# Attention part of a recurrence-plus-experts kernel: row roots one tile sooner, result additions in two pairs

## The chip, the cores and the metric

One core of a Trainium2 chip runs the whole program. Its engines are TensorE (PE in the profile, its weight loads PEld), VectorE (DVE), ScalarE (ACT), GpSimd (POOL) and SyncE (SP), each with its own queue of instructions. They meet at semaphores. PSUM holds what TensorE writes, SBUF the rest. The metric is the device time of one execution in microseconds (us).

## The reference, cut to what matters

The input x is 2 sequences of 1024 rows of 256 values, fp32. A row normalisation gives xn, and the result adds two functions of it to x:

```python
xn = _layernorm(x)
x = x + _L0_attn_ref(xn, ...) + _L0_ffn_ref(xn, ...)

def _L0_attn_ref(hidden_states, ...):
    ...                                   # a gated recurrence over time, in logarithms -> log_h
    log_h = (log_h - log_h.mean()) / jnp.std(log_h, ddof=1)
    h = jnp.exp(log_h)[:, 1:, :]
    x = h + hidden_states
    mu = x.mean(axis=-1, keepdims=True)
    var = x.var(axis=-1, keepdims=True)
    return (x - mu) * jax.lax.rsqrt(var + LN_EPS) * ln_w + ln_b

def _L0_ffn_ref(hidden_states, ...):
    ...                                   # softmax over 8 experts, each row keeps 2 of them
    for e in range(NUM_EXPERTS):
        h = jax.nn.silu(x @ w1[e].T) * (x @ w3[e].T)
        out = out + h @ w2[e].T * expert_weight
```

The last three lines of the attention part, the normalisation of the rows of h + xn, are what this change is about.

## The kernel before

**Tiles.** Each row goes to two experts. The (row, expert) pairs are sorted by expert into tiles of 128 rows, numbered from 0; between 33 and 39 tiles can be needed, 36 are here (0 to 35). Every engine walks the same tiles in a loop written out by hand for j = 1 to 32, with the attention work hung into given tiles, and then a nest of conditions (`tail`) for tiles 33 and up. The weights of an expert are split into a high and a low part. They come in four pieces: SyncE loads a piece, ScalarE rounds it to the high part (line 604), POOL subtracts to get the low part (line 424). Up to two pieces fall to a tile, by a plan computed at the start.

**One tile j on each engine.** TensorE: up products (`up`, line 1296), transposes of the next tile's rows (line 1265), in tiles 20 to 27 also transposes of a part of h (`h_back`, line 1354), down products of tile j - 1 (line 1314), transposes of the gated values (`h_tile`, line 1326, after the gate). ScalarE: silu (line 595), high part of the next rows (line 572), scaling copy of the down products of tile j - 1 out of PSUM (`y_copy`, line 621), high part of the gated values (`h_hi`, line 590), then the pieces. VectorE: `gate` (line 961, two products), low part of the next rows (line 952, the up products of tile j + 1 wait for it), `slot_weight` (line 1067), the hook `between(j)`, `h_lo` (line 956, the second half of the down products waits for it), the hook `after(j)`. `h_lo(j)` runs when the up products of tile j + 1 have already begun.

**The attention rows.** In tiles 20 to 27 VectorE adds h to xn, two groups of 128 rows to a step, and takes their mean and variance (`row_stats`). ScalarE takes square roots for four steps at a time (`row_deviations`, wrapped in two loads of an activation table, lines 696 and 704), in the second half of tiles 24 and 28. VectorE takes reciprocals (`row_scales`) in tiles 25 and 29 and runs `last_norm(m)`, m = 0 to 7, in `after` of tiles 25 to 32: four products of 128x256, two on line 1054 and two on line 1059, all operands in SBUF. They raise the semaphore s_p2 by 2.

**Adding into the result.** The result buffer starts as a copy of x. POOL adds to it: for every tile a `scatter` (line 406) of the 128 scaled rows, after `y_copy`, and four times `add_attention` (line 413), a plain transfer of 512 normalised rows that adds. Scatters and additions can touch the same rows, so each waits for all before it: `rows_added` waits for the scatters (s_st) and for the additions so far (s_ab). A tile on POOL is: the gather of the rows of tile j + 4 (line 390), the scatter of tile j - 1, then the pieces of tile j. The additions stand ahead of POOL's tiles 27, 29 and 31 and behind tile 32. The last tile's scatter is at line 467, after its own copy (line 725).

**End of TensorE's work.** Ahead of the last down products stand twelve products of constants (`warm(LAST_FILL)`, line 1176), whose result nobody reads.

Of the kernel before, what the change touches and what calls it, by code (L numbers as in the profile page):

```python
# [14 lines left out]
P = 128  # L15
# [11 lines left out]
SURE = 2 * NTOK // P + 1  # L27
# [18 lines left out]
SPLIT = 512  # L46
WARM = 96
FILL = 8
LAST_FILL = 12
BIG = 3.0e38  # L50


def build_program(nc, x, small, w_main, w_tail, out, xn_dram):
# [5 lines left out]
    with ctx:  # L59
# [285 lines left out]
        def _(pool):  # L345
# [47 lines left out]
            def rows_added(j, parts):  # L393

                if j:
                    pool.wait_ge(s_st, 16 * j)
                if j == 0:
                    pool.wait_ge(s_fill, 16)
                if parts:
                    pool.wait_ge(s_ab, 16 * parts)  # L400
# [5 lines left out]
                pool.indirect_dma_start(out, bass.IndirectOffsetOnAxis(sidx[:, j:j + 1], 0),  # L406
                                        ysb[:, j % DEEP, :], None, compute_op=ALU.add).then_inc(s_st, 16)

            def add_attention(j, m):

                pool.wait_ge(s_p2, 4 * m + 4)
                rows_added(j, m)
                pool.dma_start(out[4 * m * P:4 * (m + 1) * P, :].rearrange("(t p) d -> p t d", p=P),
                               xn[:, 4 * m:4 * m + 4, :], accum_op=ALU.add).then_inc(s_ab, 16)

            def split_due(before, j):

# [26 lines left out]
            for i in range(8):  # L444
                done = pool.value_load(plan[0:1, ds(LOOP * i + 1, 1)], min_val=0, max_val=PIECES * (E - 1))
                for u in range(LOOP):
                    j = LOOP * i + 1 + u
                    if j in (27, 29, 31):
                        add_attention(j - 1, added)
                        added += 1  # L450
                    done = tile(i, u, done, added)
            add_attention(SURE - 1, added)

            def drain(j):
                if j + DEEP < NTILES:
# [18 lines left out]
        def _(act):  # L474
# [171 lines left out]
            def row_deviations(h):  # L646
                act.wait_ge(s_p1, 3 * (4 * h + 4))
                act.activation(std[:, 8 * h:8 * h + 8], mv[:, 8 * h:8 * h + 8, 1], ACT.Sqrt,
                               bias=eps[:, :]).then_inc(s_std3, 1)
# [33 lines left out]
            def roots(j):  # L683
                if j == 18:
                    deviation()
                else:
                    row_deviations((j - 24) // 4)

            def tile(i, u, done=None, table=None, first=None, second=None):

# [18 lines left out]
            for i in range(8):  # L709
                done = act.value_load(plan[0:1, ds(LOOP * i + 1, 1)], min_val=0, max_val=PIECES * (E - 1))  # L710
                for u in range(LOOP):
                    j = LOOP * i + 1 + u
                    if j in (3, 4, 5, 6, 7, 10, 11, 12, 13, 19, 20):
                        done = tile(i, u, done, "natural_log_exp_and_others", exp_log_first, exp_log_second)
                    elif j in (18, 24, 28):
                        done = tile(i, u, done, "sqrt_and_others", None, roots)
                    else:
                        done = tile(i, u, done)
# [11 lines left out]
        def _(dve):  # L730
# [303 lines left out]
            def row_stats(m):  # L1034
                rows = xn[:, 2 * m:2 * m + 2, :]
                dve.wait_ge(s_htr, m + 1)
                dve.tensor_tensor(rows, tr_ps.rearrange("p (t d) -> p t d", t=2), rows, ALU.add).then_inc(s_p1, 1)
                dve.wait_ge(s_p1, 3 * m + 1)
                for t in range(2):
                    ins = dve.bn_stats(st3[:, t, :], xn[:, 2 * m + t, :])  # L1040
                ins.then_inc(s_p1, 1)
                dve.wait_ge(s_p1, 3 * m + 2)
                for t in range(2):
                    ins = dve.bn_aggr(mv[:, 2 * m + t, :], st3[:, t, :])
                ins.then_inc(s_p1, 1)

            def row_scales(h):
                dve.wait_ge(s_std3, h + 1)
                dve.reciprocal(rstd[:, 8 * h:8 * h + 8], std[:, 8 * h:8 * h + 8]).then_inc(s_rs3, 1)
                dve.wait_ge(s_rs3, h + 1)  # L1050

            def last_norm(m):
                for t in range(2 * m, 2 * m + 2):
                    ins = dve.scalar_tensor_tensor(xn[:, t, :], xn[:, t, :], mv[:, t, 0:1], lnwb[:, 0, :],  # L1054
                                                   ALU.subtract, ALU.mult)
                ins.then_inc(s_p2, 1)
                dve.wait_ge(s_p2, 2 * m + 1)
                for t in range(2 * m, 2 * m + 2):
                    ins = dve.scalar_tensor_tensor(xn[:, t, :], xn[:, t, :], rstd[:, t:t + 1], lnwb[:, 1, :],  # L1059
                                                   ALU.mult, ALU.add)  # L1060
                ins.then_inc(s_p2, 1)
# [31 lines left out]
            def between(j):  # L1093
                if j == 1:
                    less_n(0)
                if j == 2:
                    less_n(2)
                if j in (4, 5, 6, 7):
                    add_half(j // 2, 1 - j % 2)
                if j == 3:  # L1100
                    run_max(0)
                if j in (8, 9):
                    run_max(j - 6)
                if j in (10, 12):
                    run_scan(j - 10)
                if 13 <= j <= 16:
                    plus_max(j - 13)
                if 20 <= j <= 27:
                    row_stats(j - 20)

            def after(j):
                if j == 1:
                    add_l3(1)
                    less_n(1)
                if j == 2:
                    less_n(3)
                if j == 3:
                    max_steps(0)
                    less_max(0)
                if j == 4:  # L1120
                    run_max(1)
                if j == 5:
                    max_steps(1)
                    less_max(1)
                if j == 6:
                    add_l3(2)
                    add_l3(3)
                if j == 7:
                    less_l2(2)
                    less_l2(3)  # L1130
                if j in (8, 9):
                    max_steps(j - 6)
                    less_max(j - 6)
                if j in (11, 12):
                    run_scan(1 if j == 11 else 3)
                if 13 <= j <= 16:
                    logh(j - 13)
                    if j < 16:
                        log_stats(j - 13)
                    else:  # L1140
                        sums()
                if j == 17:
                    squares()
                if j == 18:
                    normaliser()
                if j in (25, 29):
                    row_scales((j - 25) // 4)
                if 25 <= j <= 32:
                    last_norm(j - 25)

            def tile(i, u, hooks=False):

# [18 lines left out]
        def _(pe):  # L1171
# [215 lines left out]
                    tile(i, u, True)  # L1387

            def last_down(used):
                warm(LAST_FILL)  # L1390
                down(used - 1, pe.snap(r_before, min_val=0, max_val=E - 1))
            tail(pe, tile, last_down)

# [37 lines left out]
```

## Time and profile before

| | us |
|---|---|
| median of 3 runs | 357.22 (357.09 to 359.14) |
| profiled execution | 357.79 |
| its span (first to last event in the profile) | 356.1 |
| TensorE busy | 325.8 (91%) |
| VectorE busy | 260.8 (73%) |
| ScalarE busy | 219.9 (62%) |
| POOL busy | 206.4 (58%) |
| mean granted clock of TensorE | 0.969 |

The page shares the span out over the chain of work that ended last: 54% of it is TensorE, 23% VectorE, 8% ScalarE, 2% transfers. In 40 slices of the span TensorE is busy 70% or more in the first 38, some 30% in the next and not at all in the last. The kernel moves 37.00 MB, 11.97 of them through POOL's queue.

### The profile page before, as it was taken

How to read it: one execution, taken by the hardware profiler on the slowest of the kernel's cores; microseconds unless marked ns; L12 is line 12 of the kernel's file. 1: busy time of each engine (PE TensorE's matmuls, PEld its weight loads, DVE VectorE, ACT ScalarE, POOL GpSimd, SP SyncE). 2: the span in 40 equal slices, each digit the busy share in tenths (PEclk: the TensorE clock that was granted, in tenths of full speed). 3: DMA queues.
4: the chain of work that ended last, by engine and by line, in shares of the span. 5: the costliest groups of instructions: out<-in, count | busy, mean ns of one | idle time of the engine just before them, and what ended most of it. 6: DMA issues, size and time to landing. Idle time of an engine off the chain costs nothing.

```text
span 356.1 us, 6682 instructions
## 1 busy us (share of the span) xinstructions
PE 325.8 (91%) x1964; PEld 273.9 (77%) x1964; DVE 260.8 (73%) x466; ACT 219.9 (62%) x328; POOL 206.4 (58%) x137
## 2 busy tenths in 40 slices
PE   8998999799999999999898999999999999979830
PEld 8883464588878898997787899889898988969730
DVE  5488787989996899889899842584589668763300
ACT  2547997455879974999854269934853485323400
POOL 4500023159968674989899728563885475945331
PEclk9999969989999999999999999999999999999985
DMA  7924912005444542354354434542463534354621
GB/s 263 426 120 137 293 52 59 15 11 150 122 82 115 142 101 32 80 129 129 44 144 109 102 38 115 142 101 33 84 181 89 75 45 76 47 76 49 98 38 15
DMA packets 19086, 37.00 MB, mean 104 GB/s; under 512 B 2272, under 2 KB 13536, under 8 KB 19008
## 3 DMA queue, kind: packets, MB, share of 16 engines
q0 software_dynamic: 9168, 11.97, 21.5%
q1 hardware_dynamic: 8496, 22.56, 20.4%
q10 hardware_dynamic: 1376, 1.85, 1.4%
q8 instruction: 29, 0.48, 0.6%
q14 instruction: 17, 0.14, 0.1%
HBM read 27.45 MB, written 11.03 MB: 108 GB/s over the span
## 4 chain that ended last, share of the span: by engine, by line
PE 54%; DVE 23%; ACT 8%; issue 8%; DMA 2%; ACTq 1%; POOL 1%; POOLq 0%; DVEq 0%
PE PS L1296 23%; PE PS L1314 11%; PE PS L1190 6%; PE PS L1326 5%; DVE wrow L1067 3%; DVE tmp L961 3%; PE PS L1176 2%; DMA out<-work,sidx 2%; DVE hT L956 2%; DVE U L985 2%; DVE A L998 1%; PE PS L1220 1%; DVE xrow L1054 1%; DVE xrow L1059 1%; PE PS L1265 1%
## 5 line engine op out<-in xcount | busy, mean ns | idle before, releaser
L1296 PE MATMUL PS<-wbuf,xT 128*128 128x512 f32 (+1 forms) x648 | 149.6, 384 | 4.9 <-issue 3.7
L1296 PEld LDWEIGHTS PS<-wbuf,xT 128*128 128x128 f32 x648 | 118.3, 190 | 29.4 <-issue 9.3
L424 POOL TENSOR_TENSOR wbuf<-raw,wbuf x28 | 81.4, 2924 | 23.1 <-ACT wbuf L604 21.4
L406 POOL DMA_INDIRECT out<-work,sidx x35 | 62.7, 1792 | 53.2 <-ACT work L621 20.1
L1314 PE MATMUL PS<-wbuf,hT 128*128 128x256 f32 x648 | 86.8, 288 | 0.0
L1314 PEld LDWEIGHTS PS<-wbuf,hT 128*128 128x128 f32 x648 | 79.3, 189 | 1.9 <-issue 1.9
L390 POOL DMA_INDIRECT work<-xn_dram,gidx x39 | 50.4, 1292 | 51.8 <-DVE gidx L892 36.1
L595 ACT ACTIVATE tmp<-PS 128x512 f32<-128x512 f32 x72 | 32.0, 460 | 41.6 <-PE PS L1296 41.3
L961 DVE TENSOR_TENSOR tmp<-tmp,PS 128x512 f32<-128x512 f32 x72 | 35.0, 516 | 29.4 <-ACT tmp L595 28.6
L956 DVE TENSOR_TENSOR hT<-PS,hT 128x768 fp32r<-128x768 f32 x36 | 34.2, 949 | 29.3 <-ACT hT L590 24.2
L621 ACT ACTIVATE work<-PS,wrow 128x256 f32<-128x256 f32 x35 | 16.4, 470 | 38.0 <-PE PS L1314 38.0
L1067 DVE SCALAR_TENSOR_TENSOR wrow<-work,first_pick 128x1 f32<-128x1 f32 x37 | 37.1, 1003 | 0.0
L1326 PE MATMUL PS<-ident,tmp 128*128 128x128 f32 x216 | 30.1, 275 | 5.7 <-DVE tmp L961 5.6
L590 ACT ACTIVATE hT<-PS 128x768 fp32r<-128x768 f32 x35 | 28.4, 810 | 10.4 <-PE PS L1326 10.4
L1190 PE MATMUL PS<-xnT_M,small_sb 128*128 128x512 f32 x64 | 32.3, 646 | 1.0 <-ACT tmp L525 1.0
L604 ACT ACTIVATE wbuf<-raw x28 | 30.4, 1110 | 4.0 <-issue 3.9
L1326 PEld LDWEIGHTS PS<-ident,tmp 128*128 128x128 f32 x216 | 24.0, 141 | 7.9 <-DVE tmp L961 6.9
L1190 PEld LDWEIGHTS PS<-xnT_M,small_sb 128*128 128x128 f32 x64 | 12.6, 208 | 14.1 <-issue 12.9
L704 ACT ACT_TABLE_LOAD x14 | 18.0, 1283 | 0.3
L696 ACT ACT_TABLE_LOAD x14 | 18.0, 1283 | 0.3
L952 DVE TENSOR_TENSOR xT<-PS,xT 128x256 fp32r<-128x256 f32 x37 | 15.5, 419 | 0.1
L572 ACT ACTIVATE xT<-PS 128x256 fp32r<-128x256 f32 x37 | 14.0, 381 | 1.7 <-PE PS L1265 1.7
(185 smaller groups left out, 350.7 us busy)
## 6 DMA issues: line engine op xcount, KB each, us to landing
raw<-w_main SPq DMA_DIRECT2D x24, 544.0 KB
raw<-w_main SPq DMA_DIRECT2D x8, 416.0 KB
xn_dram<-xrow SPq DMA_DIRECT2D x4, 516.0 KB, 7.2
out<-xrow POOLq DMA_DIRECT2D x4, 512.0 KB, 6.1
xrow<-x SPq DMA_DIRECT2D x4, 256.0 KB, 4.8
xrow<-x ACTq DMA_DIRECT2D x4, 256.0 KB, 5.4
small_sb<-small ACTq DMA_DIRECT2D x1, 768.0 KB, 7.9
work<-xn_dram,gidx POOLq DMA_INDIRECT x39
```

The costliest lines, as they stand in the source:

```text
L390: pool.indirect_dma_start(xg[:, k, :], None, xn_dram, bass.IndirectOffsetOnAxis(gidx[:, j:j + 1], 0)).then_inc(s_gt[k], 16)
L406: pool.indirect_dma_start(out, bass.IndirectOffsetOnAxis(sidx[:, j:j + 1], 0), ysb[:, j % DEEP, :], None, compute_op=ALU.add).then_inc(s_s ...
L424: pool.tensor_tensor(lo, raw[:, ds(part, WP)], hi.bitcast(fp32), ALU.subtract).then_inc(s_w, 1)
L595: act.activation(sls[n], w1_ps[n], ACT.Silu).then_inc(s_silu, 1)
L604: act.activation(wslot(p // PIECES + 1, 0, part), raw[:, ds(part, WP)], ACT.Copy).then_inc(s_hi, 1)
L956: dve.tensor_tensor(hT[:, 1, :], hT_ps, hT[:, 0, :].bitcast(fp32), ALU.subtract).then_inc(s_hlo, 1)
L961: dve.tensor_tensor(g_hs[n], sls[n], w3_ps[n], ALU.mult).then_inc(s_g, 1)
L1067: dve.scalar_tensor_tensor(wrow[:, j:j + 1], xg[:, k, D:D + 1], first_pick[:, j:j + 1], xg[:, k, D + 1:D + 2], ALU.mult, ALU.max).then_inc ...
L1190: ins = pe.matmul(PS[:, base + qo * CH:base + (qo + 1) * CH], wzh_sb[:, q, mat, qo * P:(qo + 1) * P], xnT[:, q, c * CH:(c + 1) * CH], star ...
L1296: ins = pe.matmul(PS[:, at:at + cols], xT[:, slot, xpart, q * P:(q + 1) * P], wbuf[:, w, wpart, q * 2 * F + at:q * 2 * F + at + cols], sta ...
L1314: ins = pe.matmul(y_ps, hT[:, hpart, c * P:(c + 1) * P], wbuf[:, w, wpart, W13 + c * D:W13 + (c + 1) * D], start=(c == 0 and hpart == 0 an ...
L1326: ins = pe.transpose(hT_ps[:, c * P:(c + 1) * P], g_h[:, a:a + P], ident[:, :])
```

## The change

The roots, reciprocals and `last_norm` steps 0 to 5 move one tile forward. Step 6 goes into `between(30)`, ahead of `h_lo(30)`, and step 7 into `after(30)`. Tiles 31 and 32 carry no step any more. POOL issues the additions in two pairs, ahead of its tiles 28 (steps 0 to 3) and 31 (steps 4 to 7), each pair with one wait in front and none between; the addition behind tile 32 goes. The twelve constant products go.

```diff
-LAST_FILL = 12
...
-            def add_attention(j, m):
-
-                pool.wait_ge(s_p2, 4 * m + 4)
-                rows_added(j, m)
-                pool.dma_start(out[4 * m * P:4 * (m + 1) * P, :].rearrange("(t p) d -> p t d", p=P),
-                               xn[:, 4 * m:4 * m + 4, :], accum_op=ALU.add).then_inc(s_ab, 16)
+            def add_attention(j, first):
+
+                pool.wait_ge(s_p2, 4 * first + 8)
+                rows_added(j, first)
+                for m in (first, first + 1):
+                    pool.dma_start(out[4 * m * P:4 * (m + 1) * P, :].rearrange("(t p) d -> p t d", p=P),
+                                   xn[:, 4 * m:4 * m + 4, :], accum_op=ALU.add).then_inc(s_ab, 16)
...
-                    if j in (27, 29, 31):
+                    if j in (28, 31):
                         add_attention(j - 1, added)
-                        added += 1
+                        added += 2
                     done = tile(i, u, done, added)
-            add_attention(SURE - 1, added)
...
-                    row_deviations((j - 24) // 4)
+                    row_deviations((j - 23) // 4)
...
-                    elif j in (18, 24, 28):
+                    elif j in (18, 23, 27):
                         done = tile(i, u, done, "sqrt_and_others", None, roots)
...
                 if 20 <= j <= 27:
                     row_stats(j - 20)
+                if j == 30:
+                    last_norm(6)
...
-                if j in (25, 29):
-                    row_scales((j - 25) // 4)
-                if 25 <= j <= 32:
-                    last_norm(j - 25)
+                if j in (24, 28):
+                    row_scales((j - 24) // 4)
+                if 24 <= j <= 29:
+                    last_norm(j - 24)
+                if j == 30:
+                    last_norm(7)
...
             def last_down(used):
-                warm(LAST_FILL)
                 down(used - 1, pe.snap(r_before, min_val=0, max_val=E - 1))
```

## Rows read from the trace of the kernel before

**Rows 1.** Timeline, last 35 us: start, length, engine, line, operation, [idle before <-releaser].

```profile
322.67 1.58 POOL L406 DMA_INDIRECT out<-work,sidx  x1 [1.26 <-DMA out<-work,sidx]
...
327.09 1.38 POOL L413 DMA_DIRECT2D out<-xrow  x1 [2.84 <-DMA out<-work,sidx]
...
333.73 1.64 POOL L406 DMA_INDIRECT out<-work,sidx  x1 [3.88 <-issue]
...
338.99 0.84 PE L1176 MATMUL PS<-ones_b 128*128 128x128 bf16 x12 [2.32 <-issue]
...
342.11 0.47 ACT L725 ACTIVATE hst<-PS,wrow 128x256 f32<-128x256 f32 x1 [3.61 <-PE PS L1314]
343.00 1.56 POOL L406 DMA_INDIRECT out<-work,sidx  x1 [2.44 <-DMA out<-work,sidx]
...
347.79 1.57 POOL L467 DMA_INDIRECT out<-hst,scol  x1 [2.67 <-DMA out<-work,sidx]
```

**Rows 2.** Timeline: POOL's weight pieces (L424) and VectorE's products beside them.

```profile
265.97 3.23 DVE L1059 SCALAR_TENSOR_TENSOR xrow<-xrow,rstd,small_sb 128x256 f32<-128x256 f32 x2
265.99 2.53 POOL L424 TENSOR_TENSOR wbuf<-raw,wbuf  x1 [0.57 <-issue]
...
289.39 5.24 POOL L424 TENSOR_TENSOR wbuf<-raw,wbuf  x2
...
308.10 3.12 POOL L424 TENSOR_TENSOR wbuf<-raw,wbuf  x1
308.15 3.75 DVE L1054 SCALAR_TENSOR_TENSOR xrow<-xrow,mv,small_sb 128x256 f32<-128x256 f32 x2
```

**Rows 3.** Timeline: up products (L1296) of tiles 26, 27, 30, 32, 33; gate; normalisation.

```profile
262.77 4.10 PE L1296 MATMUL PS<-wbuf,xT 128*128 128x512 f32 x18
...
269.12 0.94 DVE L961 TENSOR_TENSOR tmp<-tmp,PS 128x512 f32<-128x512 f32 x2
...
270.86 4.11 PE L1296 MATMUL PS<-wbuf,xT 128*128 128x512 f32 x18
...
280.16 0.87 DVE L1054 SCALAR_TENSOR_TENSOR xrow<-xrow,mv,small_sb 128x256 f32<-128x256 f32 x2
...
292.13 4.12 PE L1296 MATMUL PS<-wbuf,xT 128*128 128x512 f32 x18
...
306.15 4.11 PE L1296 MATMUL PS<-wbuf,xT 128*128 128x512 f32 x18
...
315.85 4.10 PE L1296 MATMUL PS<-wbuf,xT 128*128 128x512 f32 x18 [1.50 <-issue]
```

**Rows 4.** Timeline: copies (ACT L621), scatters (L406) and gathers (L390) of tiles 22 to 34.

```profile
247.81 0.47 ACT L621 ACTIVATE work<-PS,wrow 128x256 f32<-128x256 f32 x1 [2.17 <-PE PS L1314]
...
249.09 1.58 POOL L406 DMA_INDIRECT out<-work,sidx  x1 [4.41 <-ACT work L621]
...
277.79 0.47 ACT L621 ACTIVATE work<-PS,wrow 128x256 f32<-128x256 f32 x1 [2.17 <-PE PS L1314]
...
288.02 1.57 POOL L406 DMA_INDIRECT out<-work,sidx  x1 [2.55 <-DMA out<-work,sidx]
...
305.74 1.01 POOL L390 DMA_INDIRECT work<-xn_dram,gidx  x1 [0.17 <-DVE wrow L1067]
...
307.05 1.58 POOL L406 DMA_INDIRECT out<-work,sidx  x1 [0.30 <-issue]
```

**Rows 5.** Windows: length, busy by engine (x instructions), granted clock, DMA share, GB/s.

```profile
70.00:71.00 1.00, 0.45 (x2) 0.41 (x3) 0.97 (x2) 0.00 (x0) 0.00 (x0) 1.00 0.00 0
...
70.55:76.21 5.66, 5.66 (x18) 4.38 (x18) 0.70 0.01 3
278.16:282.25 4.09, 4.09 (x18) 3.23 (x18) 1.00 0.84 144
```

In the first of these the engines are PE, PEld, DVE, ACT and POOL; the other two count the up products (L1296) of tiles 1 and 28 alone, on PE and PEld.

**Rows 6.** Window while one addition (L413, issued at 327.09) moves.

```profile
331.00:331.50 0.50, 0.50 (x3) 0.39 (x3) 0.50 (x1) 0.00 (x0) 0.00 (x0) 1.00 1.22 197
```

**Rows 7.** Page, groups by line: h_lo, count, busy us and mean ns.

```profile
L956 DVE TENSOR_TENSOR hT<-PS,hT 128x768 fp32r<-128x768 f32 x36 | 34.2, 949 | 29.3 <-ACT hT L590 24.2
```

## The prediction

> **What bounds the kernel now.** I read the chain of waits first, then the timeline of the last 110 us engine by engine, then parts of that stretch in windows. From tile 20 on the kernel is a chain of tiles of about 7 us on TensorE: the up products of tile 28 begin at 278.16 [rows 5] and those of tile 30 at 292.13 [rows 3], two tiles in 13.97. In the last 14 us it is another chain. POOL adds rows to the result one transfer at a time, each waiting for the one before. The last partial attention transfer goes out at 327.09, the next scatter only at 333.73, and from there scatter follows scatter until the last one at 347.79 [rows 1]. Tile 35, the last, was copied out of PSUM by 342.11 + 0.47 = 342.58 [rows 1], so its rows lie 5.2 us waiting for their turn. That gap is what the change can win.
>
> The second thing to see is how VectorE and POOL block each other. POOL's subtraction for a weight piece (line 424) ran from 265.99, and beside it two products of the last normalisation (line 1059) took 3.23, where two of the same size (line 1054 at 280.16 [rows 3]) took 0.87. At 308.10 and 308.15 the same: line 1054 stood until the piece was done, 3.75 for its two products [rows 2]. Both kinds of instruction read two SBUF operands; VectorE products with one operand in PSUM ran through such a piece undisturbed. So every step of the normalisation that falls on a piece costs up to 3.1 us of VectorE time. The gate (line 961) of the next tile is queued behind it, the transposes wait for the gate, and TensorE for both: U(j), the start of the up products of tile j, came 270.86 - 269.12 = 1.74 after that gate began [rows 3]. Before, this cost about 8.09 - 7.30 = 0.8 in tile 26 (262.77 to 270.86, where the next tile took 7.30 [rows 3, 5]), and in tile 32 (306.15 to 315.85, 9.70, of which 1.50 is another wait [rows 3]) 9.70 - 6.98 - 1.50 = 1.2.
>
> **The change part by part.** *Roots one tile sooner.* ScalarE's two table loads and the root move from tiles 24 and 28 to 23 and 27. Nothing is added. In tile 23 they stand in front of two weight pieces, as they do in tile 28 now, and there the up products of tile 30 show no wait [rows 3]. I cost this at 0; what covers it is the transposes of h that TensorE does in tile 24. If that cover failed, the gate of tile 24 would be late, and I bound it by what a late gate cost in tile 26, 0.8.
>
> *Normalisation one step sooner.* Step 0 moves from tile 25 to 24, where no piece is running. Step 1 then stands where step 0 stood, against the piece at 265.99. I carry the 0.8 of tile 26 over: 0 change, bounds -0.8 (it misses) and +1.0 (three of its four products remain, not two).
>
> *Two pieces at a time, ahead of tile 28.* On POOL the wait moves from tiles 27 and 29 to tile 28. Behind it in POOL's queue stand the gather of tile 32, the scatter of tile 27 and, behind these, the two weight pieces of tile 28, which before ran at 289.39 [rows 2]. Their new time:
> - The copy of tile 26 ends at 277.79 + 0.47 = 278.26, and a scatter follows its copy by 249.09 - 248.28 = 0.81 [rows 4]: 279.07.
> - An add follows the scatter it waits for by 327.09 - 322.67 = 4.42 [rows 1]: 283.49. Step 3 of the normalisation, which it waits for too, is done by 282.
> - The next scatter follows one add by 333.73 - 327.09 = 6.64 [rows 1]. No row shows two adds. Below, the second hides altogether (6.64 in all); above, both stand in line (13.3). While one add moves, the windows show 197 GB/s with all engines busy [rows 6], so 0.524 MB more takes 2.66. I take 9.30, nearer the lower bound, because the rest of an add is latency that overlaps: 292.79.
> - The pieces begin 289.39 - 288.02 = 1.37 after the scatter and last 5.24 [rows 2, 4]: from 294.16 to 299.40. Call this A.
>
> The Trainium skill, "DMA: Bandwidth & Descriptors", section "Anatomy of one DMA — SWDGE (gpsimd) path", prices a transfer at about 2.0 us and its bytes at 436 GB/s; by that the second add would take 1.2, A would begin 1.46 sooner, and the time below would be 358.6 (estimate from that page). The trace's 197 GB/s for an add into the result disagrees, and the sum goes by the trace.
>
> VectorE reaches a normalisation 280.16 - 278.16 = 2.00 after U of the tile [rows 3, 5], so step 5 in tile 30 is due at 292.13 + 2.00 = 294.13, on the start of A. One product of four gets in at most; the other three (0.44 each) follow A. The gate of tile 30 comes at 299.40 + 1.4 = 300.8 and U(31) at 302.5; it was 7 us after 292.13.
>
> *Steps 6 and 7 both in tile 30.* Step 6 now stands ahead of h_lo(30), step 7 behind it. POOL meanwhile runs on: after A a gap of some 0.2 (estimate), a gather to scatter distance of 307.05 - 305.74 = 1.31 [rows 4], then 1.05 to the next piece [rows 2, 4]. Piece B runs from 301.96 to 305.08 (3.12 as at 308.10), piece C, by the same steps, from 307.64 to 310.76. Step 6 is due between 300.8 and 302.5, so it falls on B and ends at 305.08 + 1.8 = 306.9. h_lo, 0.95 [rows 7], ends at 307.8. Step 7 is due at 307.8, just behind the start of C: it ends at 310.76 + 1.8 = 312.6. That is when the gate of tile 31 can begin, and U(32) = 314.3. Before it was 306.15: +8.2. The bounds: if step 6 or 7 slips one or two products in ahead of its piece, 0.4 to 0.9 less at each; if A comes behind step 5, the third rival.
>
> *Nothing after tile 30.* Tile 32 has no step any more, so its 1.2 goes: -1.2. TensorE is then 7.0 late at the end.
>
> *Tail.* The addition behind tile 32 and its wait go: scatter follows scatter from tile 30 on. The pair ahead of tile 31 starts once step 7 is done, at 312.9, and its scatter at 322.2; five more steps of 4.4 to 4.8 end at 344.2 to 346.2. The last copy ends at 342.58 + 7.0 = 349.6, so TensorE's chain ends last now. The twelve constant products stand between 338.99 and the last down products [rows 1]: at most 0.84 to win, at least 0; I take 0.3, since the waits they covered stay. The last scatter goes out 0.3 to 0.8 after its copy: 349.8, against 347.79 [rows 1]. The 8.3 from there to the end of the span stay. Difference: +2.0.
>
> *The clock.* The gaps in front of the transposes of tiles 30 and 31 are 3 us and more. Early in the kernel, when TensorE had been busy for only 0.45 of the us from 70 to 71, the granted clock fell behind it: the up products from 70.55 on ran at 0.70 on average (partly at 1.2 GHz) and took 5.66, against 4.09 at the full 2.4 GHz [rows 5]. The loss of 1.57 behind the first gap is hidden by the second; behind the second it can count. I add half, 0.8; bounds 0 and 1.57.
>
> Sum: 0 + 8.2 - 1.2 - 0.3 + 0.5 - 5.2 + 0.8 = +2.8. The profiled execution took 357.79 with a span of 356.1 and 1.7 around it; the changed kernel would take 360.6. Its median lies 0.57 below that: 357.22 + 2.8 = 360.0.
>
> **The rivals.** *First: the pieces miss the normalisation (ends faster).* If steps 5 to 7 fall between the pieces, TensorE loses nothing and the scatter chain alone counts. The pair ahead of tile 31 then starts 4.42 after the scatter of tile 29 at 306.6, so at 311.0; its scatter comes at 320.3 and five steps end at 342.3 to 344.3, 3.5 to 5.5 earlier than 347.79: 352.7. For it: margins at B and C are a few tenths. Against it: A is 5.24 long and a tile has only 7, and three meetings must all fail. The point from which it decides: A beginning after 295.9 and C after 309.6.
>
> *Second: the clock stays down (slower still).* If the clock falls in both gaps and again ahead of the last down products, which now follow a gap of over 2.3 with no constant products in it, tile 32 pays 1.57 and the last products up to 2.4: 363.5. For it: the early fall, and the 2.32 of idle time ahead of 338.99 [rows 1]. Against: all three gaps would have to count in full, and the one ahead of 338.99 is there before as well.
>
> *Third: A comes late.* If the two adds take 11 or more in place of 9.3, step 5 is done ahead of A, tile 31 begins on time, step 6 follows A and only step 7 stands behind B: U(32) comes 3.5 sooner, 356.5. For it: the upper bound of 13.3 for the pair. Against: 197 GB/s.
>
> *Fourth: the constant products do nothing,* because the sequencer was busy anyway: 0.3 more, inside the range.
>
> The Trainium skill, "SBUF — State Buffer", section "Who interferes with whom", states the rule that would bring the slow outcome: a VectorE instruction with two SBUF inputs and a GpSimd one that reads SBUF exclude each other for a whole instruction, and issue order decides. The rows at 265.99 and 308.10 agree (2.4 and 2.9 us of standing).
>
> **How the numbers follow.** The forecast, three meetings with half a loss of clock (358.5 to 361.5), has 0.45; the late A 0.20; the slow clock 0.18; the miss 0.17. The range from 353.0 to 363.0 cuts about half of each outer case. A measurement of this kernel can tell about 1% from no change, here 3.6: faster than 353.6 is the miss, 0.17. Slower than 360.8 is the slow clock and a third of the forecast, 0.33. Within 1% is the rest, 0.50.
>
> **What would show it.** Right, if in the profile after: line 413 has two issues side by side near 283.5 and 313; the two pieces behind the first pair run from 294 to 299, with a line 1054 or 1059 of several us beside them; transposes (line 1326) of tiles 30 and 31 wait for line 961 by 3 us each; the last scatter follows the last copy within 1 us. Wrong, if line 1054 and 1059 keep 0.48 each behind 290 (the miss), if the first scatter behind the pair comes after 294.5 (late A), or if the scatters are still back to back at the end.

## The result and the profile after

| | before | after |
|---|---|---|
| median of 8 runs each, side by side | 357.26 us | 361.25 us |
| lowest and highest | 357.00 to 359.14 | 360.25 to 362.75 |
| ratio after / before (95% interval) | | 1.0107 (1.0081 to 1.0133) |
| profiled execution, its span | 357.79, 356.1 | 361.65, 359.8 |

The change made the kernel slower by 4.0 us, just over the 1% that the prediction took for what can be told apart. The forecast of 360.0 us is 1.25 us too low; the time lies in its range. The ratios of this document count the runs that lie within 1.5% of the fastest of their kernel; the medians count all.

Here are the rows of the changed kernel that answer to [rows 1 to 3]. In it the scatter is line 405, the adds 413, the weight pieces 424, the normalisation 1053 and 1058, slot_weight 1066, the gate 960, the up products 1299, the down products 1317, the transposes of the gated values 1329 and the last copy 724. First POOL and the last copy, from the timeline (start, length, engine, line, operation, operands, count, [idle before <-releaser]):

```profile
283.64 2.73 POOL L413 DMA_DIRECT2D out<-xrow  x2 [2.77 <-DMA out<-work,sidx]
293.50 1.65 POOL L405 DMA_INDIRECT out<-work,sidx  x1 [5.76 <-issue]
294.69 5.47 POOL L424 TENSOR_TENSOR wbuf<-raw,wbuf  x2
302.69 3.10 POOL L424 TENSOR_TENSOR wbuf<-raw,wbuf  x1
308.44 3.08 POOL L424 TENSOR_TENSOR wbuf<-raw,wbuf  x1
313.42 2.73 POOL L413 DMA_DIRECT2D out<-xrow  x2 [1.91 <-DVE xrow L1058]
323.06 1.63 POOL L405 DMA_INDIRECT out<-work,sidx  x1 [5.52 <-issue]
...
350.33 0.47 ACT L724 ACTIVATE hst<-PS,wrow 128x256 f32<-128x256 f32 x1 [4.47 <-PE PS L1317]
351.58 1.57 POOL L466 DMA_INDIRECT out<-hst,scol  x1 [4.75 <-ACT hst L724]
```

The 283.64 line is the first pair of adds, the three lines of L424 are the weight pieces A, B and C of the prediction, those of tiles 28, 29 and 30. The last scatter now leaves 351.58 - 350.80 = 0.78 behind the end of the last copy, where before it came 5.2 behind [rows 1]: the queue at the end is gone. What was lost stands on VectorE, in the same 30 us (timeline, VectorE):

```profile
294.98 5.87 DVE L1058 SCALAR_TENSOR_TENSOR xrow<-xrow,rstd,small_sb 128x256 f32<-128x256 f32 x2
300.77 0.94 DVE L960 TENSOR_TENSOR tmp<-tmp,PS 128x512 f32<-128x512 f32 x2
301.96 3.85 DVE L1066 SCALAR_TENSOR_TENSOR wrow<-work,first_pick 128x1 f32<-128x1 f32 x1
308.31 3.89 DVE L1053 SCALAR_TENSOR_TENSOR xrow<-xrow,mv,small_sb 128x256 f32<-128x256 f32 x2
313.04 0.95 DVE L960 TENSOR_TENSOR tmp<-tmp,PS 128x512 f32<-128x512 f32 x2
```

Step 5 stands beside A (5.87 for two products that take 0.87 alone), slot_weight beside B (3.85 for one column), step 7 beside C (3.89). Behind them the gates of tiles 30 and 31 begin at 300.77 and 313.04. TensorE follows, and its clock falls behind each gap (timeline, TensorE, tiles 31 to 33 and the last tile; then windows: length, busy us of PE, PEld, DVE, ACT, POOL, granted clock, DMA share, GB/s):

```profile
301.50 1.38 PE L1329 MATMUL PS<-ident,tmp 128*128 128x128 f32 x6 [2.98 <-DVE tmp L960]
302.65 5.23 PE L1299 MATMUL PS<-wbuf,xT 128*128 128x512 f32 x18
313.78 0.88 PE L1329 MATMUL PS<-ident,tmp 128*128 128x128 f32 x6 [3.55 <-DVE tmp L960]
314.80 5.65 PE L1299 MATMUL PS<-wbuf,xT 128*128 128x512 f32 x18
323.21 4.10 PE L1299 MATMUL PS<-wbuf,xT 128*128 128x512 f32 x18
346.54 3.70 PE L1317 MATMUL PS<-wbuf,hT 128*128 128x256 f32 x18 [2.50 <-issue]
```

```profile
302.00:304.00 2.00, 2.00 (x8) 1.65 (x7) 2.00 (x2) 0.81 (x1) 2.00 (x2) 0.50 0.41 74
316.00:318.00 2.00, 2.00 (x6) 1.52 (x6) 0.49 (x1) 0.00 (x0) 1.24 (x2) 0.50 1.16 160
347.00:349.00 2.00, 2.00 (x11) 2.00 (x11) 0.00 (x0) 0.00 (x0) 0.00 (x0) 0.50 0.45 59
```

Tile 32's up products begin 8.65 later than before (306.15 [rows 3]), the last scatter leaves 3.79 later.

### The profile page after: what moved, and what is told of

The parts are those of the page before. It is cut to its first block, busy times and chain, and to the rows that moved or that the text cites. A ratio compares the mean times of both kernels' runs of the same rounds, so it can differ in the third digit from the quotient of the medians.

```text
span 359.8 us, 6656 instructions
## 1 busy us (share of the span) xinstructions
PE 327.3 (91%) x1952; PEld 275.6 (77%) x1952; DVE 267.0 (74%) x466; ACT 219.6 (61%) x328; POOL 205.7 (57%) x137
## 3 DMA queue, kind: packets, MB, share of 16 engines
q10 hardware_dynamic: 1376, 1.85, 1.4%
## 4 chain that ended last, share of the span: by engine, by line
PE 43%; DVE 35%; ACT 9%; issue 7%; DMA 3%; ACTq 1%; POOL 0%; DVEq 0%; POOLq 0%
PE PS L1299 19%; PE PS L1317 11%; DVE wrow L1066 5%; PE PS L1193 4%; PE PS L1329 4%; DVE tmp L960 4%; DVE hT L955 3%; DVE xrow L1053 3%; DVE xrow L1058 3%; DMA out<-work,sidx 2%; DVE U L984 2%; DVE A L997 1%; PE PS L1260 1%; DVE A L914 1%; PE PS L1223 1%
## 5 line engine op out<-in xcount | busy, mean ns | idle before, releaser
L424 POOL TENSOR_TENSOR wbuf<-raw,wbuf x28 | 82.4, 2965 | 23.1 <-ACT wbuf L603 22.3
L1317 PE MATMUL PS<-wbuf,hT 128*128 128x256 f32 x648 | 88.2, 290 | 2.5 <-issue 2.5
L1317 PEld LDWEIGHTS PS<-wbuf,hT 128*128 128x128 f32 x648 | 80.7, 192 | 4.6 <-issue 4.6
L1193 PE MATMUL PS<-xnT_M,small_sb 128*128 128x512 f32 x64 | 31.1, 626 | 1.7 <-ACT tmp L524 1.0
```

The costliest lines, as they stand in the source:

```text
L424: pool.tensor_tensor(lo, raw[:, ds(part, WP)], hi.bitcast(fp32), ALU.subtract).then_inc(s_w, 1)
L1193: ins = pe.matmul(PS[:, base + qo * CH:base + (qo + 1) * CH], wzh_sb[:, q, mat, qo * P:(qo + 1) * P], xnT[:, q, c * CH:(c + 1) * CH], star ...
L1317: ins = pe.matmul(y_ps, hT[:, hpart, c * P:(c + 1) * P], wbuf[:, w, wpart, W13 + c * D:W13 + (c + 1) * D], start=(c == 0 and hpart == 0 an ...
```

## The experiments

Two theories stood against each other in the first series. By the first, the loss is three meetings of a weight piece with a VectorE instruction that reads two tensors from SBUF; the clock adds to it and the tail gives back a part. By the second, everything behind the paired adds is late for the pair's own sake, or TensorE's clock is the loss. Every ratio below is to the kernel before run beside it on the same chip (medians 356.48, 357.43 and 357.58 us in the three series), so ratios are to be compared, not microseconds. Line numbers shift by a few between variants. The diffs are cut to the lines that matter.

### The changed kernel again (a_same)

No edit.

> The changed kernel once more, unaltered, for a second trace of it and for comparison with the runs beside it. Theory (all three long steps are systematic): the same holds, with the paired instructions behind the piece of tile 28 over 5 us and those behind the piece of tile 30 over 3 us, the up products of tile 32 at about 314 us, and the ratio 1.011 to the kernel before. What is open is the last tile's down products, 3.70 us at a granted clock of 0.50 in the first trace, while the spread-out variant without the constants had 2.38 us there at full clock. If the missing constants make the clock fall, it falls again; if it was this one execution, they take 2.38 us and the span is about 358.4.

Measured: 360.52 us, ratio 1.0084 (1.0044 to 1.0124). Timeline:

```profile
294.19 6.13 DVE L1058 SCALAR_TENSOR_TENSOR xrow<-xrow,rstd,small_sb 128x256 f32<-128x256 f32 x2
301.44 3.87 DVE L1066 SCALAR_TENSOR_TENSOR wrow<-work,first_pick 128x1 f32<-128x1 f32 x1
307.81 3.88 DVE L1053 SCALAR_TENSOR_TENSOR xrow<-xrow,mv,small_sb 128x256 f32<-128x256 f32 x2
314.30 5.65 PE L1299 MATMUL PS<-wbuf,xT 128*128 128x512 f32 x18 [0.16 <-issue]
345.92 2.38 PE L1317 MATMUL PS<-wbuf,hT 128*128 128x256 f32 x18 [2.41 <-issue]
349.64 1.57 POOL L466 DMA_INDIRECT out<-hst,scol  x1 [3.34 <-ACT hst L724]
```

The three meetings recur to within 0.3 us, and so does the fall of the clock in tile 32. The fall at the last down products does not: here they take 2.38 without any constant product ahead of them. So the slow last products of the first trace are no fixed part of the change.

### The constants (a_warm, b_nowarm)

The changed kernel with the constants back, and the kernel before without them.

```diff
+LAST_FILL = 12
...
 def last_down(used):
+    warm(LAST_FILL)
     down(used - 1, ...)
```

> The changed kernel with the 12 constant products put back ahead of the last tile's down products, and nothing else. Theory: of the 3.8 us that the last scatter came later, about 0.85 is the constants' absence. Their absence took 0.47 off TensorE's queue (from the last transposes' end to the last down products 2.50 us in place of 2.97), but these products then ran at a granted clock of 0.50 and took 3.70 us in place of 2.38. Put back, they give 361.3 - 1.32 + 0.47 = about 360.4 us, with the last down products near 2.4 us. Rival: the clock falls there whatever stands ahead of these products, because TensorE's earlier gap brings it down; then the products stay at 3.7 us and the time is 361.3 + 0.5 = 361.8 us.

> The kernel before without the 12 constant products ahead of the last down products, nothing else. So far the last down products ran at half clock in two of five traces without the constants and in two of five with them, so the constants do not decide it. Theory: the constants are worth nothing here, both for that and because the last scatter of this kernel follows the scatter ahead of it and not the last copy: ratio 1.000 within 0.3%. Rival: without them the last products are slow in most executions, and the copy comes 1.3 us later, which the 5.2 us between copy and scatter hide as well; then the last products' 3.7 us in the trace tells it, and the ratio is 1.000 too.

Measured: a_warm 360.42 us, ratio 1.0141 (1.0092 to 1.0189) where the changed kernel had 1.0107 and 1.0084: no gain, and the expected 0.85 us does not show. b_nowarm 357.29 us, ratio 1.0007 (0.9977 to 1.0037): nothing. The last down products took 2.38 or 2.39 us in some traces and 3.5 or more in others, either way: of five traces with the constants two show the longer time (b_sooner 3.51; in a_gapfill the last eight of 18 took 2.08, at half clock), of eight without them four (after, a_lnpsum_ts, a_early, a_early_only). So the a_warm theory falls: what decides over the clock there was not found, but it is not these twelve products alone. The traces without them do sort by the idle time ahead of the last down products: 2.23 to 2.41 us in the four at full clock, 2.50 to 2.96 in the four that took 3.5 us or more. With the constants the order is another (2.32 ahead of them in before, at full clock; 1.97 and 2.09 in b_sooner and a_gapfill), and no run set this idle time on purpose. Their removal is worth nothing that these runs can tell.

### Weight and bias in PSUM (a_lnpsum, b_lnpsum)

Bank 7 is free from tile 28 on. ScalarE copies the normalisation's weight and bias there, and steps 4 to 7 take them from it; they then read one tensor from SBUF in place of two. The order on GpSimd's queue stays.

```diff
+def ln_to_psum(j):                 # ScalarE, tile 28 (29 in b_lnpsum)
+    act.wait_ge(s_p1, 24)
+    act.activation(ln_ps, lnwb, ACT.Copy).then_inc(s_lnp, 1)
 def last_norm(m):
+    ln = lnwb
+    if m >= 4:
+        dve.wait_ge(s_lnp, 1)
+        ln = ln_ps
-    ... mv[:, t, 0:1], lnwb[:, 0, :], ...
+    ... mv[:, t, 0:1], ln[:, 0, :], ...
```

> The changed kernel, in which ScalarE copies the normalisation's weight and bias to PSUM at tile 28 (bank 7, free by then), and steps 4 to 7 of the normalisation read them there; all else, GpSimd's order too, is the same. Theory: the loss is in steps 5 and 7, whose two instructions lasted 5.87 us beside the weight pieces of tile 28 (GpSimd 5.47 us for two) and 3.89 us beside that of tile 30, where without a piece they take under 1 us. An operand in PSUM takes these steps out of the pieces' way: the up products of tile 31 start at about 299.3 in place of 302.65 and those of tile 32 at about 308.5 in place of 314.80 (slot_weight, which reads SBUF alone, is still held by the piece of tile 29, and step 6 stands behind it). The end follows them: 361.3 - 6.3 = 355 us (353 to 357). Rival: the steps are late because all that stands behind the paired transfer is late, or because VectorE and GpSimd hold each other up whatever the operand's place; then the long instructions stay and the time is 361 us, or 361.5 with ScalarE's copy.

> The kernel before, with the same copy of weight and bias to PSUM (ScalarE, at tile 29) and normalisation steps 4 to 7 reading them there. Theory: in the kernel before a long step delays a gate as well (tile 32's, 2.8 us), but the last scatter comes 5.2 us behind the last copy there, at the end of a row of scatters and adds on GpSimd's queue, so that TensorE being sooner by 2.8 us moves little: 357.3, at most 0.5 us less. What the copy to PSUM does by itself is thus about 0, and a gain of the same copy in the changed kernel is not a gain that any kernel has of it. Rival: the end of the kernel before still follows TensorE (the scatters wait for copies), and it gains about 2.8 us: 354.5 us.

Measured: a_lnpsum 353.69 us, ratio 0.9934 (0.9906 to 0.9962), faster than both kernels. Timeline (pieces are L426 here, normalisation 1065 and 1070, slot_weight 1078, up products 1311, scatter 407):

```profile
295.03 0.87 DVE L1070 SCALAR_TENSOR_TENSOR xrow<-xrow,rstd,PS 128x256 f32<-128x256 f32 x2
295.51 5.53 POOL L426 TENSOR_TENSOR wbuf<-raw,wbuf  x2
297.25 3.81 DVE L1078 SCALAR_TENSOR_TENSOR wrow<-work,first_pick 128x1 f32<-128x1 f32 x1
299.00 4.09 PE L1311 MATMUL PS<-wbuf,xT 128*128 128x512 f32 x18
303.53 0.86 DVE L1065 SCALAR_TENSOR_TENSOR xrow<-xrow,mv,PS 128x256 f32<-128x256 f32 x2
303.57 3.09 POOL L426 TENSOR_TENSOR wbuf<-raw,wbuf  x1
304.43 0.87 DVE L1070 SCALAR_TENSOR_TENSOR xrow<-xrow,rstd,PS 128x256 f32<-128x256 f32 x2
307.04 4.11 PE L1311 MATMUL PS<-wbuf,xT 128*128 128x512 f32 x18 [0.21 <-issue]
...
339.54 0.47 ACT L732 ACTIVATE hst<-PS,wrow 128x256 f32<-128x256 f32 x1 [2.99 <-PE PS L1329]
344.82 1.57 POOL L468 DMA_INDIRECT out<-hst,scol  x1 [2.61 <-DMA out<-work,sidx]
```

Step 7 runs 0.86 and 0.87 across a piece. Tile 31 starts on time, tile 32 at 307.04 (expected 308.5). slot_weight, still two tensors from SBUF, is held for 3.81, by A and not by the piece of tile 29 that the expectation named. TensorE has no gap of 3 us any more and the clock stays at 1.00. The last scatter now waits for the scatter ahead of it and leaves 4.8 us behind the last copy: the bound is POOL's row of transfers again. In the kernel before the same copy brings 0.9972 (0.9946 to 0.9997), 1.0 us, a little more than the half us expected, and the rival's 2.8 us does not come. So in the changed kernel it is worth about 5.4 us (1.0084 to 0.9934), in the kernel before 1.0: the difference, some 4 us (give or take 2, by the three intervals), is what the change lost to the meetings that the copy takes away, those of steps 5 and 7.

### slot_weight with per-row scalars (a_lnpsum_ts)

The edit of a_lnpsum, and this one:

```diff
-dve.scalar_tensor_tensor(wrow[:, j:j + 1], xg[:, k, D:D + 1], first_pick[:, j:j + 1],
-                         xg[:, k, D + 1:D + 2], ALU.mult, ALU.max)
+dve.tensor_scalar(wrow[:, j:j + 1], xg[:, k, D:D + 1], first_pick[:, j:j + 1],
+                  xg[:, k, D + 1:D + 2], ALU.mult, ALU.max)
```

> The changed kernel with the normalisation's weight and bias in PSUM from step 4 on, and slot_weight written as a tensor_scalar with its two other operands as per-row scalars, in place of a scalar_tensor_tensor with two tensors from SBUF. In the version without this last edit slot_weight still lasted 3.81 us beside the piece of tile 29 (GpSimd 5.53 us for the two), and cost the up products of tile 32 about 1.2 us. Theory (what is held beside a weight piece is an instruction with two tensor operands in SBUF): slot_weight takes 0.2 us everywhere, the up products of tile 32 start 1.2 us sooner; but the end now follows the row of scatters behind the second pair of adds, so the time falls by 0.5 at most: 353.2 us where the version without it had 353.7. Rival (any VectorE instruction on SBUF alone is held): slot_weight still takes 3.8 us, and nothing changes.

Measured: 353.93 us, ratio 0.9913 (0.9881 to 0.9945). Timeline:

```profile
293.97 5.51 POOL L426 TENSOR_TENSOR wbuf<-raw,wbuf  x2
296.33 0.27 DVE L1078 TENSOR_SCALAR wrow<-work,first_pick 128x1 f32<-128x1 f32 x1
305.50 4.09 PE L1311 MATMUL PS<-wbuf,xT 128*128 128x512 f32 x18 [0.33 <-POOL wbuf L426]
343.86 1.57 POOL L468 DMA_INDIRECT out<-hst,scol  x1 [2.64 <-DMA out<-work,sidx]
```

The same three SBUF addresses, one as a tensor and two as per-row scalars, cost 0.27 in the middle of A. So reading SBUF is not enough to be held. In a_lnpsum the normalisation's instruction stayed the same, and with one tensor in PSUM it was not held; together this points to the second tensor operand in SBUF. (Here the instruction's kind changes along with its operands.) TensorE is sooner, so much that the up products of tile 32 now wait 0.33 for the weight piece itself; the time stays, for the row of scatters ends the kernel.

### Steps 6 and 7 one a tile (a_spread)

```diff
-if j == 30: last_norm(6)           # ahead of h_lo
-if 24 <= j <= 29: last_norm(j - 24)
-if j == 30: last_norm(7)
+if 24 <= j <= 31: last_norm(j - 24)
-if j in (28, 31): add_attention(...)
+if j in (28, 32): add_attention(...)
```

> The changed kernel with normalisation steps 6 and 7 behind tiles 30 and 31, one a tile as the steps before them, in place of both in tile 30; the second pair of adds stands ahead of tile 32 in place of tile 31. Theory: step 6 stands behind the 31st tile's h_lo and only the piece of tile 30 can hold it, so one gate is late by 3 us in place of two together by 8: up products of tile 31 still at about 302.7, of tile 32 at about 310.6 in place of 314.80, and the second pair of adds, which now waits for step 7 one tile later, still ends before the last copies. Time 361.3 - 4.2 = about 357 us, or 355 where the late pair leaves no queue at the end. Rival: the pair one tile later makes the row of scatters behind it end later, and what TensorE gives back the row takes: 361 us or more. Rival: the loss is with the first pair alone (tile 30's gate), then 361 us as well.

Measured: 357.90 us, ratio 1.0029 (0.9998 to 1.0059), some 2 us better than the changed kernel. Timeline:

```profile
294.25 5.73 DVE L1058 SCALAR_TENSOR_TENSOR xrow<-xrow,rstd,small_sb 128x256 f32<-128x256 f32 x2
306.64 4.25 DVE L1058 SCALAR_TENSOR_TENSOR xrow<-xrow,rstd,small_sb 128x256 f32<-128x256 f32 x2
312.74 5.11 PE L1295 MATMUL PS<-wbuf,xT 128*128 128x512 f32 x18
```

Three instructions still meet the three pieces; only the last of them is step 6 and not step 7, so the gate of tile 31 comes 2 us sooner, not 4. Tile 32 starts at 312.74, expected 310.6.

### The normalisation sooner, alone (b_sooner)

The kernel before with `row_deviations((j - 23) // 4)`, roots in tiles 23 and 27, scales in 24 and 28, and steps 0 to 7 behind tiles 24 to 31.

> The kernel before with only the row deviations, the scales and the normalisation one tile sooner (steps 0 to 7 behind tiles 24 to 31), the four adds and the constants as before. Theory: no step meets a piece that it did not meet, except that step 7, behind tile 31, takes the place of step 6 beside the piece of tile 30; the gate of tile 32 is late as before, and the last scatter is set by the row of adds and scatters, whose last add waits at the end of the loop for its queue and not for step 7: within 0.5 us of the kernel before. Then the changed kernel's loss is from the paired adds, which move the pieces, and from steps 6 and 7 in one tile. Rival: the sooner normalisation by itself costs what the changed kernel lost, 3 to 4 us.

Measured: 358.22 us, ratio 1.0030 (1.0002 to 1.0058), about 1.1 us. Timeline:

```profile
288.71 3.17 DVE L1059 SCALAR_TENSOR_TENSOR xrow<-xrow,rstd,small_sb 128x256 f32<-128x256 f32 x2
288.80 5.45 POOL L424 TENSOR_TENSOR wbuf<-raw,wbuf  x2 [0.74 <-ACT wbuf L604]
```

More steps meet pieces than expected (4 and 6, and slot_weight). TensorE waits only 0.55 and 0.41 for the two late gates, but these tiles, 29 and 31, take 8.12 and 7.87 where an undisturbed one takes 6.86. By itself the sooner normalisation costs about a third of what the whole change does, with an interval from 0.1 to 2.1 us.

### TensorE's gaps filled (a_gapfill)

```diff
+GAPS = {30: 48, 31: 52}
+if hooks and j in GAPS:            # ahead of h_tile(j)
+    warm(GAPS[j])
 h_tile(j)
```

and the 12 constants at the end.

> The changed kernel with constant products in TensorE's two gaps: 48 ahead of tile 30's transposes of h, 52 ahead of tile 31's, and the 12 back ahead of the last down products. It takes no wait away, it only keeps TensorE busy in it. Theory: the granted clock then stays at 1.00 in tiles 31 and 32; tile 31's up products take 4.1 us in place of 5.23, but tile 31's gate is late for VectorE's sake and takes that up; tile 32's take 4.1 in place of 5.65, and that 1.55 us comes off the end: 361.3 - 1.55 = 359.7 us, and up to 0.85 more where the last down products ran at half clock: 358.9 us. So the clock is at most 2.4 of the 7 us by which TensorE was late, and the steps are the rest. Rival (the clock is the loss): about 356 us.

Measured: 361.87 us, ratio 1.0109 (1.0069 to 1.0148); no gain in the time. Timeline:

```profile
302.99 4.11 PE L1301 MATMUL PS<-wbuf,xT 128*128 128x512 f32 x18 [0.28 <-issue]
315.17 4.11 PE L1301 MATMUL PS<-wbuf,xT 128*128 128x512 f32 x18
322.58 4.11 PE L1301 MATMUL PS<-wbuf,xT 128*128 128x512 f32 x18 [0.31 <-issue]
348.58 2.08 PE L1319 MATMUL PS<-wbuf,hT 128*128 128x256 f32 x8 [0.61 <-issue]
```

With the gaps filled the up products of tiles 31 and 32 run at full clock, 4.11 in place of 5.04 to 5.65. From tile 31 to 32 nothing is won (12.18 against 314.30 - 302.17 = 12.13 in a_same): VectorE sets that gate. Tile 32 takes 322.58 - 315.17 = 7.41 against 322.71 - 314.30 = 8.41. So the clock behind the second gap costs 1.0 us, not 1.55. In this execution the last products gave it back at half clock, and the intervals can't tell 1 us. What falls is the rival: the clock is not the loss.

### The pieces ahead of the waiting scatter (a_early, a_early_only)

In tile 28 the two pieces ready on ScalarE's side wait on POOL's queue behind a scatter that waits for the pair. The edit puts them ahead of it; a_early has it with the two edits of a_lnpsum_ts, a_early_only alone.

```diff
 gather(j + DEEP)
+if early:                          # j == 28
+    done = split_due(done, j)
+    scatter(j - 1, parts)
+    return done
 scatter(j - 1, parts)
```

> The changed kernel with weight and bias in PSUM, slot_weight as a tensor_scalar, and in tile 28 the two weight pieces put ahead of the scatter that waits for the first pair of adds, in place of behind it. Theory: in that kernel no gate is late any more and the end is set by the row of scatters; the pieces (5.5 us) stood idle behind the pair's landing, though ScalarE's halves of them were ready 4.7 us before (288.1 against the scatter's 292.8). Ahead of it they run while the pair lands. The scatter of tile 28 then comes about 3.7 us sooner, that of tile 29 only 1.5, since it waits for its copy; the second pair and the rest follow by 1.5: 353.9 - 1.5 = 352.4 us, ratio 0.987. Rival: the pieces delay the scatter and nothing is gained (ratio 0.991 as without the edit).

> The changed kernel with that last edit alone: in tile 28 the two weight pieces ahead of the scatter that waits for the pair; weight, bias and slot_weight in SBUF as they were. Theory (what costs is where a piece lies against VectorE's instructions with two SBUF tensors): the two pieces now lie at about 288 to 294 and meet slot_weight of tile 28 (a 3 to 5 us instruction in place of 0.2) and no more step 5, so that tile 30's gate is late by 1 us at most; the pieces of tiles 29 and 30 still meet slot_weight and steps 6 or 7. Up products of tile 31 about 300.5 in place of 302.65, of tile 32 311 to 313 in place of 314.8; time 357 to 359 us. Rival (any order of the pieces costs the same, since they all have to be run beside VectorE): 360.5 us as the changed kernel.

Measured: a_early 351.62 us, ratio 0.9828 (0.9783 to 0.9874), the fastest of all; a_early_only 357.08 us (351.88 to 358.70), ratio 0.9937 (0.9891 to 0.9983). This last ratio counts six of twelve runs; the median of all twelve is 0.9986 of the kernel before's (357.08 / 357.58), and the traced execution, of 358.01 us, is not among the six. Timeline of a_early:

```profile
289.27 5.03 POOL L426 TENSOR_TENSOR wbuf<-raw,wbuf  x2 [0.93 <-ACT wbuf L609]
298.56 1.59 POOL L407 DMA_INDIRECT out<-work,sidx  x1 [1.10 <-DMA out<-work,sidx]
309.43 2.72 POOL L415 DMA_DIRECT2D out<-xrow  x2 [1.08 <-issue]
342.07 1.57 POOL L472 DMA_INDIRECT out<-hst,scol  x1 [3.16 <-ACT hst L736]
```

Timeline of a_early_only:

```profile
288.55 3.16 DVE L1062 SCALAR_TENSOR_TENSOR xrow<-xrow,rstd,small_sb 128x256 f32<-128x256 f32 x2
300.40 4.10 PE L1303 MATMUL PS<-wbuf,xT 128*128 128x512 f32 x18
304.21 4.40 DVE L1057 SCALAR_TENSOR_TENSOR xrow<-xrow,mv,small_sb 128x256 f32<-128x256 f32 x2
311.20 5.66 PE L1303 MATMUL PS<-wbuf,xT 128*128 128x512 f32 x18
```

In a_early the scatter of tile 28 leaves 14.32 behind the issue of the pair (298.56 - 284.24), where it was 18.14 in a_lnpsum_ts (300.97 - 282.83): 3.8 sooner, as expected. The second pair comes 2.9 sooner by the same count, where 1.5 was expected, and the last scatter follows the last copy by 0.8 again: TensorE's chain ends last once more. In a_early_only A meets step 4 (3.16) and then holds slot_weight for 1.25, where 3 to 5 us of slot_weight were expected, but the tiles start where expected (300.40 and 311.20). Moving one pair of pieces some 6 us within a tile (288.83 in place of 294.69), with no work taken away, brings a kernel 1% slower than before back to its time; whether it is faster than the kernel before, these runs leave open. The rival, that any order of the pieces costs the same, is out: it asked for 360.5, and none of the twelve runs took more than 358.70.

## Why the prediction was right, and where its terms were off

The mechanism is shown, the time was right to 1.25 us, and the ratio of 1.0107 lies just outside the 1% that was held likeliest, with 1.0084 for the second series just inside it. Term by term, from the traces of before and after:

| term | predicted | measured | from |
|---|---|---|---|
| tile 32's start | +8.2 | +8.65 | 314.80 - 306.15 |
| tile 32's late gate gone | -1.2 | -2.84 | 9.70 before, 6.86 for an undisturbed tile |
| clock in tile 32 | +0.8 | +1.55 | 8.41 - 6.86 |
| constants | -0.3 | -0.47 | 2.97 to 2.50 ahead of the last down products |
| clock at the last down products | 0 (second rival) | +1.32 | 3.70 - 2.38 |
| end | -4.7 | -4.43 | copy to last scatter, 5.21 to 0.78 |
| sum | +2.8 | +3.78 | 351.58 - 347.79 = 3.79 |

That the sum is right to 1 us is in part luck: tile 32's gate gave back 1.64 more than it was priced at, and the clock took 0.75 and 1.32 more. The 1.32 is missing in a_same, where the same difference is 349.64 - 347.79 = 1.85; so a pair of traces settles the sum to no better than 2 us.

- **Roots and steps 0, 1.** Priced at 0. Tile 27 starts at 271.06 in after and at 270.86 before [rows 3]. That held; but b_sooner shows that the sooner steps are not free as a whole, 1.1 us (0.1 to 2.1), in tiles that the prediction counted under the pair.
- **The pair.** 283.64 (283.49 predicted); to the next scatter 9.86, not 9.30. The prediction's 6.64 for one add is the shortest of four; the longest is 282.49 - 275.44 = 7.05. So the add beside another costs 2.8 to 3.2, a little over the 2.66 from the windows' rate. The Trainium skill, "DMA: Bandwidth & Descriptors", section "Anatomy of one DMA — SWDGE (gpsimd) path", would have it at 1.2 (estimate from that page); the runs disagree. The third rival needed a scatter behind 294.5; it came at 293.50, and A met step 5 in after, a_same, a_warm, a_spread and a_gapfill alike.
- **A, B, C.** A from 294.69 to 300.16 (294.16 to 299.40 predicted), gate 300.77 (300.8), U(31) 302.65 (302.5). That the gate was on time is two misses that cancel: A ended 0.76 late, but two products of step 5 got in ahead of it, not one, and the gate came 0.6 behind A, not 1.4. B met slot_weight, which stands ahead of step 6, and not step 6: the prediction did not name this instruction, though it reads two columns from SBUF as the normalisation reads two tensors, and was held in the kernel before too (3.22 from 291.44). The result for step 6 is the same, its end at 307.52 where 306.9 was forecast. C met step 7: gate 313.04 (312.6), U(32) 314.80 (314.3). a_lnpsum and a_lnpsum_ts show the cause: with one tensor fewer from SBUF each of these instructions is short beside the same pieces (0.87 and 0.27). The Trainium skill, "SBUF — State Buffer", section "Who interferes with whom", has this rule; the 0.87 with one operand in PSUM agrees with it.
- **Tile 32's -1.2 was mis-sized.** The prediction set aside 1.50 of the 9.70 as another wait that would stay, TensorE's wait at the entry of the tail [rows 3]. It went as well: tile 32 takes 6.86 plus what the clock costs. With the clock kept up (a_gapfill) the tile takes 7.41, so some half a us of the wait comes back when TensorE is fast; together the tile gave 9.70 - 8.41 = 1.29, for 1.2 - 0.8 = 0.4 forecast.
- **The clock.** Taking half for tile 32 was too little in the sum's own terms (1.55), about right by a_gapfill (1.0). The second rival's 363.5 holds only with the 0.3 of the constants dropped as well; its two terms alone give 363.2. It added the last down products: they ran at half clock in the first trace and at full clock in the second, and the constants, which that rival blamed, have no part in it. The fourth rival, that the constants do nothing, is what the runs show.
- **The first rival** (the pieces miss, 352.7, last scatter at 342.3 to 344.3) did not come, but a_lnpsum_ts makes its condition true by other means: no gate is late, and the last scatter leaves at 343.86, so the tail was rightly read.

What stays open: how the 1.1% splits between the pair and steps 6 and 7 in one tile. b_sooner is at 1.003 with neither, a_spread at 1.003 with the pairs and the steps apart, and the meetings differ in each. And why the clock falls at the last down products in some executions.

## What to carry to other kernels

When a change moves a transfer on a queue, list what stands behind it on that queue and lay those pieces against the neighbour engine's instructions: here the price was less the transfer than the subtractions behind it that landed on normalisation steps. Before moving work in time, see whether the conflict can be taken away where it arises: one operand in PSUM and two as per-row scalars made the same order 0.9% faster than the kernel before instead of 1% slower. And work that is ready does not belong behind a wait: putting the two pieces ahead of the waiting scatter brought the rest, 351.6 us.

## What the runs showed of the hardware

- Whether a waiting VectorE instruction gets in between two weight pieces varies. In after, a_same, a_spread and a_warm it stood through both (rows of 5.87, 6.13, 5.73 and 6.19 us), in b_sooner and a_early_only through one (3.17 and 3.16). The start of the row does not tell: those of b_sooner and a_early_only began 0.1 and 0.3 ahead of the first piece, but that of a_warm 0.4 ahead of it as well (293.08 and 293.49). The Trainium skill, "SBUF — State Buffer", section "Who interferes with whom", says that the order of issue decides; what decides between two queued pieces was not settled here.
- A scalar operand taken per row from SBUF did not count as a second tensor: 0.27 us for slot_weight inside a piece, 3.81 with two tensors.
- Two adds issued together into the result took 9.6 to 10.8 us to the next scatter (9.86 and 9.64 in after, 10.81 in a_early), one alone 6.64 to 7.05 in the kernel before.
- The granted clock was 0.50, that is 1.2 GHz, behind gaps of 2.98 and 3.55 us in TensorE's work; it stayed at 1.00, 2.4 GHz, when constant products filled them (a_gapfill) and behind a gap of 0.52 (a_lnpsum).
